# Two-layer relational graph network with a mixture-of-experts tail: the first node stage's side work moved to other steps

## The chip, the core and the metric

The kernel runs on one core of a Trainium2 chip. The core has five engines that run their own instruction streams and meet by semaphores: PE (TensorE, matrix products and transposes), DVE (VectorE), ACT (ScalarE), POOL (GpSimd) and SP (SyncE, which here only issues DMAs). SBUF is the on-chip memory of 128 partitions, PSUM the banks that PE writes. The metric is the device time of one execution in microseconds (us).

## The reference

Two relational graph convolutions over 10000 nodes of width 512 and 5000 edges, then an expert layer over each node. Cut to what matters:

```
def rgcn_gate_layer(x, row, col, edge_type, basis, att, gate_w, root, bias):
    w = jnp.einsum('rb,bio->rio', att, basis)          # 2 relations from 30 bases
    x_j = x[col]
    msgs = []
    for r in range(2):
        gate = jax.nn.sigmoid(x_j @ gate_w[r, :, 0])
        msgs.append(gate[:, None] * x_j @ w[r])
    msg = jnp.where((edge_type == 0)[:, None], msgs[0], msgs[1])
    agg = jax.ops.segment_sum(msg, row, num_segments=x.shape[0])
    return agg + x @ root + bias

n = layernorm(x)
h = relu(rgcn_gate_layer(n, src, dst, ..., layer 1)); x = x + rgcn_gate_layer(h, ..., layer 2)
x = x + experts(layernorm(x))                          # 2 shared, 8 routed (top 2)
```

## The kernel before

The kernel has five stages: node stage A, edge stage B (layer 1), node stage C, edge stage D (layer 2), and the expert stage in groups of 512 rows. Every product is made of three single-pass products of high and low parts, so each matrix operand is split: ACT writes the high part (`th`, `wrh`, `eh`), DVE the rest (`tl`, `wrl`, `el`).

**A node stage** has 79 steps, one for 128 rows (a tile). In step k of stage A, PE transposes tile k+1 (L1055), then multiplies tile k by `root` (twelve matmuls of 512 columns, L1035). ACT writes `th` of tile k+1 and the normalised `xn_a` of tile k+2. DVE writes `tl` of tile k+1 (L1309), adds the bias to the product of tile k-1 (`yout`, L1324) and takes the moments of tile k+4 (L1296); in odd steps it also aggregates the moments of a pair of tiles (L1300), from which POOL makes the scale and shift (`rstd`, `nmr`, function `pair_rstd`, L689 to L694) that ACT needs for `xn_a`. Stage C is the same without moments and scale. PE's product of tile k needs `tl` of tile k and the `yout` of tile k-2, whose PSUM bank it takes.

**Relation weights** are formed inside the node stages: in each odd step up to 63, PE combines the bases (`w_rows`, L1106), ACT copies the result out (`wevac`, L880), and SP loads the next 896 KB of bases and every fourth step stores the rows to DRAM. Behind the last store SP loads all of them as `wrl` (2048 KB, L517), and ACT and DVE split them, eight pieces, one each in steps 70 to 77 (`w_hi`, `w_lo`, L884 and L1375).

**An edge stage** has 21 pairs of 128 edge slots, sorted by relation. A pair runs through a pipeline: POOL gathers rows (`gx`, L738), DVE takes their moments (`edge_stats`, L1332), POOL makes the root (`edge_root`, L761), DVE the shift (`edge_shift`), ACT `xn_e`, DVE the gate's dot product (`edge_gate`, L1352), ACT the sigmoid and `eh`, DVE `el` (L1360), PE the turn (`edge_turn`, L1068: a product with the matrix `same` that adds edges with the same target and transposes at once) and the product with the relation's weights, ACT the message `msg`, POOL an adding scatter into DRAM (L753). Each scatter of a pair waits until those of the pair before have landed, because two pairs can hit the same row. The next node stage starts when all have landed.

The pipeline is filled inside the node stage: `lead_in` names node steps in which ACT and DVE also do a `pair_step(u)` with a negative u; -4 is the first with work (moments of pair 0), -3 adds the gate of pair 0 and moments of pair 1, -2 adds `same` and `el` of pair 0, -1 the turn of pair 0. Before they are at steps 72, 74, 76 and 78 (step 70 is in the list with u = -5, which has no work). A `pair_step` stands behind the node step's own work on each engine, so what waits in it holds the node step after it.

**Side work of stage A**: edge slots are sorted by records scattered to DRAM (POOL, 40 indirect DMAs). The slots' row numbers are then turned by PE (step 56), copied by DVE (57), stored and loaded again as one row in all partitions (`row_src`, POOL, 1344 KB, L732), and in steps 64 to 77 DVE compares three of 42 slots a step against those before (`find_repeats`, L1394), which `scatter_rows` (step 78) makes into the scatter's row numbers.

The order on each engine is the order of the code. `walk` writes steps 0 to 7 out, runs a loop of eight steps a round up to step 55, and writes the rest out; only written-out steps can carry side work. Buffers around the change: `yout` has two pairs of tiles, `xin` four, `basis_t` two.

Of the kernel before, what the change touches and what calls it, by code (L numbers as in the profile page):

```python
# [61 lines left out]
def gnn_moe_kernel(nc, x, src, dst, etype, basis, att, gate_w, root, bias,  # L62
# [21 lines left out]
    CS = P // 4  # L84
    TRASH = N
# [14 lines left out]
    with ctx:  # L100
# [356 lines left out]
        def _(sp):  # L457
# [26 lines left out]
            def step(st):  # L484
# [25 lines left out]
                if st.t.i is None and st.t.k == 2 * CS + 1:  # L510


                    for i in range(2):
                        sp.wait_ge(s_wst[i], 64 * (CS // 4) * (st.layer + 1))
                    if st.layer:
                        sp.wait_ge(s_mm, C0)
                    sp.dma_start(wrl[:, :, :].bitcast(F32), w_dram[st.layer].rearrange("m i o -> i m o")).then_inc(s_wl, 16)  # L517
# [117 lines left out]
        def _(pool):  # L635
# [88 lines left out]
            for g in range(pairs_done + 2, 31):  # L724
# [3 lines left out]
            pair_rstd(Pos(31))  # L728
# [48 lines left out]
            for g in range(32, NG - 1):  # L777
                pair_rstd(Pos(g))
            for u in range(3):
                gather(Pair(SB, u))  # L780
            for g in range(NG - 1, NG + 1):
                pair_rstd(Pos(g))
            for u in range(-4, 0):
# [38 lines left out]
        def _(act):  # L822
# [59 lines left out]
            def w_hi(layer, m):  # L882
                act.wait_ge(s_wl, 16 * (layer + 1))
# [29 lines left out]
            def step(st):  # L913
# [9 lines left out]
                if st.t.i is None:  # L923
# [3 lines left out]
                    if 70 <= st.t.k < 78:  # L927
                        w_hi(st.layer, st.t.k - 70)
# [98 lines left out]
        def _(pe):  # L1027
# [82 lines left out]
            def step(st):  # L1110
                a1 = later(st, 1)
                lead = lead_in(st)
                if st.phase == SA and st.t.i is None and st.t.k == 56:
# [129 lines left out]
        def _(dve):  # L1243
# [180 lines left out]
            def step(st):  # L1424
# [8 lines left out]
                if st.t.i is None:  # L1433
# [3 lines left out]
                    if st.phase == SA and st.t.k == 57:  # L1437
                        dve.wait_ge(s_turned, 1)
                        dve.tensor_copy(src_row16[:], bank[7][0:ET, 0:P]).then_inc(s_row16, 1)
                    if st.phase == SA and st.t.k == 64:  # L1440
# [3 lines left out]
                    if st.phase == SA and st.t.k == 78:  # L1444
                        scatter_rows()
                    if 70 <= st.t.k < 78:
                        w_lo(st.layer, st.t.k - 70)
# [196 lines left out]
```

## Time and profile before

| | us |
|---|---|
| median of 3 runs | 1728.37 |
| the runs | 1728.41, 1728.37, 1724.84 |
| the profiled execution | 1723.27 |
| its span in the trace | 1721.5 |
| PE busy | 1592.3 (92% of the span) |
| DVE busy | 914.5 (53%) |
| ACT busy | 724.4 (42%) |
| POOL busy | 504.7 (29%) |

The shares are means over all stages; a stage must be read from its own stretch of the trace. On the trace's clock stage A runs up to some 340 us, edge stage B to some 530, stage C to 828, stage D to some 1010 and the expert stage to the end. Releasers (what a wait ended with) are inferred from semaphore events, and "issue" is time in which an engine waited for nothing that the profile shows. On POOL, which issues the indirect DMAs, a wait for a landed DMA can appear so.

### The profile page before, as it was taken

To read this page: it belongs to the slowest core of one execution; us is meant where nothing else is said; L and a number is where in the kernel's file an instruction comes from. 1 tells how busy PE (TensorE), PEld (TensorE's weight loads), DVE (VectorE), ACT (ScalarE), POOL (GpSimd) and SP (SyncE) were. 2 spreads that over 40 slices of the span, in tenths; PEclk is the share of its full clock that TensorE was granted. 3 is DMA by queue.
4 is the path that set the end of the run, shared out by engine and by line. 5 is a ranking of instruction groups with operands and counts; after the bars stand their busy time and mean duration, and the time that the engine had idled before them with its cause. 6 is when DMAs were issued, how large, how long until landed. Compare 5 with 4: busy or idle time off the path is not lost. (4 is left out here: it accounts for less than half of the span.)

```text
span 1721.5 us, 24584 instructions
## 1 busy us (share of the span) xinstructions
PE 1592.3 (92%) x7903; PEld 1257.1 (73%) x7903; DVE 914.5 (53%) x2179; ACT 724.4 (42%) x1168; POOL 504.7 (29%) x559
## 2 busy tenths in 40 slices
PE   3998999798995999999999927999999999999998
PEld 2776777677783777777888715888888888888887
DVE  4554556877751333334755535556555654655543
ACT  2443444466651222222665515344444444444442
POOL 3682212457752000000467533112211311221100
PEclk9999999899997999999999958999999999999999
DMA  8998998367766999995777660132123112311201
GB/s 256 262 268 236 279 270 300 104 160 125 125 95 187 277 272 283 278 278 193 235 127 128 104 160 25 74 133 88 74 92 129 74 73 98 122 73 74 86 25 43
DMA packets 72234, 270.46 MB, mean 157 GB/s; under 512 B 12438, under 2 KB 12452, under 8 KB 57042
## 3 DMA queue, kind: packets, MB, share of 16 engines
q1 hardware_dynamic: 51714, 223.82, 40.5%
q0 software_dynamic: 20432, 45.57, 14.6%
q8 instruction: 42, 0.69, 0.2%
q14 instruction: 46, 0.38, 0.1%
HBM read 179.82 MB, written 89.48 MB: 156 GB/s over the span
## 5 line engine op out<-in xcount | busy, mean ns | idle before, releaser
L811 POOL TENSOR_TENSOR zr<-zr,xr 128x2048 f32<-128x2048 f32 (+1 forms) x19 | 89.2, 4695 | 395.4 <-DMA xr<-in_x 394.9
L839 ACT ACTIVATE th<-bank 128x512 fp32r<-128x512 f32 x158 | 94.4, 597 | 202.3 <-PE bank L1055 199.5
L1306 DVE SCALAR_TENSOR_TENSOR tl<-bank,th 128x512 fp32r<-128x512 f32 x79 | 54.6, 691 | 212.9 <-ACT th L839 212.9
L1035 PE MATMUL bank<-tth,w1h 128*128 128x512 f32 (+1 forms) x400 | 163.9, 410 | 0.1
L1035 PE MATMUL bank<-ttl,w1h 128*128 128x512 f32 (+1 forms) x400 | 156.4, 391 | 0.0
L1035 PE MATMUL bank<-w2h,gth 128*128 128x512 f32 x395 | 155.5, 394 | 0.5 <-DVE gtl L1520 0.3
L1035 PE MATMUL bank<-tth,w1l 128*128 128x512 f32 (+1 forms) x400 | 155.3, 388 | 0.0
L1035 PE MATMUL bank<-w2h,gtl 128*128 128x512 f32 x395 | 154.7, 392 | 0.0
L1035 PE MATMUL bank<-w2l,gth 128*128 128x512 f32 x395 | 154.3, 391 | 0.0
L1035 PE MATMUL bank<-root1h,th 128*128 128x512 f32 x316 | 134.8, 427 | 7.7 <-DVE yout L1324 7.1
L738 POOL DMA_INDIRECT gx<-y,dst_slot x42 | 46.2, 1100 | 301.9 <-ACT xn_e L857 286.6
L1035 PE MATMUL bank<-root2h,th 128*128 128x512 f32 x316 | 131.9, 418 | 0.6 <-issue 0.6
L1035 PE MATMUL bank<-root1l,th 128*128 128x512 f32 x316 | 127.2, 403 | 0.0
L1035 PE MATMUL bank<-root1h,tl 128*128 128x512 f32 x316 | 126.5, 400 | 0.0
L1035 PE MATMUL bank<-root2l,th 128*128 128x512 f32 x316 | 125.1, 396 | 0.0
L1035 PE MATMUL bank<-root2h,tl 128*128 128x512 f32 x316 | 123.9, 392 | 0.0
L1309 DVE TENSOR_TENSOR tl<-bank,th 128x512 fp32r<-128x512 f32 x79 | 54.5, 690 | 120.2 <-ACT th L839 120.2
L880 ACT ACTIVATE wevac<-bank 128x512 f32<-128x512 f32 x64 | 38.3, 598 | 186.8 <-PE bank L1106 184.2
L969 ACT ACTIVATE gel<-bank,b 128x512 f32<-128x512 f32 (+1 forms) x100 | 68.4, 684 | 106.9 <-PE bank L1035 106.8
L1324 DVE TENSOR_TENSOR yout<-bank,bias_b 128x512 f32<-128x512 f32 x158 | 107.4, 680 | 1.6 <-DMA y<-yout 1.6
L1068 PE MATMUL bank<-same,eh 128*128 128x256 f32 x336 | 85.1, 290 | 15.2 <-issue 10.3
L1520 DVE TENSOR_TENSOR gtl<-gsc,gth 128x512 fp32r<-128x512 f32 (+1 forms) x80 | 85.3, 1066 | 21.7 <-ACT gth L981 16.3
(201 smaller groups left out, 3790.6 us busy)
## 6 DMA issues: line engine op xcount, KB each, us to landing
basis_t<-in_gnn_basis SPq DMA_DIRECT2D x64, 896.0 KB
xin<-in_x SPq DMA_DIRECT2D x39, 512.0 KB
y<-yout SPq DMA_DIRECT2D x39, 512.0 KB
xin<-y SPq DMA_DIRECT2D x39, 512.0 KB
z<-yout SPq DMA_DIRECT2D x39, 512.0 KB
xr<-in_x SPq DMA_DIRECT2D x19, 1024.0 KB, 6.9
zr<-z SPq DMA_DIRECT2D x19, 1024.0 KB, 4.8
out<-zr SPq DMA_DIRECT2D x19, 1024.0 KB, 3.9
```

Source lines behind the costliest of these rows:

```text
L738: pool.indirect_dma_start(out=gx[:, e % 6, :], out_offset=None, in_=x if pr.phase == SB else y1, in_offset=bass.IndirectOffsetOnAxis(ap=ds ...
L811: pool.tensor_tensor(zq, zq, xr[:, q.mod(2), 0:n, :], ALU.add).then_inc(s_zx, 1)
L839: act.activation(th_a[:, s, :], tpb[s][:], f).then_inc(s_hi, 1)
L880: act.activation(wevac[:, u.mod(2), c.mod(2), :], wb[c.mod(2)][:], ACT.Copy).then_inc(s_wv, 1)
L969: act.activation(gel[:, u % 2, 0:n], outb[u % 2][:, 0:n], ACT.Gelu, bias=b1[:, c:c + 1]).then_inc(s_ge, 1)
L1035: ins = pe.matmul(out_ap, a(k), b(k), start=first, stop=last)
L1068: pe.matmul(o, eh[:, j, k * P:(k + 1) * P], m, start=j == 0, stop=False)
L1306: ins = dve.scalar_tensor_tensor(out=tl_a[:, s, :], in0=tpb[s][:], scalar=0.0, in1=th_a[:, s, :].bitcast(F32), op0=ALU.max, op1=ALU.subtract)
L1309: ins = dve.tensor_tensor(tl_a[:, s, :], tpb[s][:], th_a[:, s, :].bitcast(F32), ALU.subtract)
L1324: dve.tensor_tensor(yout[:, st.gg.mod(2), st.t.mod(2), :], outb[st.T.mod(2)][:], bias_b[st.layer][:], ALU.add).then_inc(s_y, 1)
L1520: dve.tensor_tensor(gtl[:, c, 0:n], source, gth[:, c, 0:n].bitcast(F32), ALU.subtract).then_inc(s_gl, 1)
```

## The change

All of it is in stage A and its like in stage C (same functions):

- row numbers are turned at step 34 and copied at 35; POOL's waits for them move with it, from pair 31's `pair_rstd` to pair 20's;
- repeats are compared in steps 42 to 55, `scatter_rows` is at 56;
- the leading steps of the edge pipeline are 59, 63, 67 and 78; POOL's first six gathers stand ahead of pair 31's `pair_rstd`;
- `wrl` is loaded in two parts, rows 0 to 111 at step 61 and the rest at 65, and split two pieces a step in steps 68 to 71;
- the loops end at step 31, so steps 32 to 55 are written out.

```
-            if st.t.i is None and st.t.k >= NT - 9 and (NT - 1 - st.t.k) % 2 == 0:
-                return (SB if st.phase == SA else SD), -1 - (NT - 1 - st.t.k) // 2
+            left = NT - 1 - st.t.k
+            if st.t.i is None and left in LEADS:      # {19: -4, 15: -3, 11: -2, 0: -1}
+                return (SB if st.phase == SA else SD), LEADS[left]
...
-            stop = 2 * CS - 8
+            stop = CS
...
-                if st.t.i is None and st.t.k == 2 * CS + 1:
+                if st.t.i is None and st.t.k in (2 * CS - 3, 2 * CS + 1):
+                    first, last = (0, EARLY) if st.t.k < 2 * CS else (EARLY, CS)
                     for i in range(2):
-                        sp.wait_ge(s_wst[i], 64 * (CS // 4) * (st.layer + 1))
+                        sp.wait_ge(s_wst[i], 64 * (CS // 4 * st.layer + last // 4))
...
-            for g in range(pairs_done + 2, 31):
+            turn_g = TURN_AT // 2 + 3
+            for g in range(pairs_done + 2, turn_g):
                 pair_rstd(Pos(g))
...
+            first_g = turn_g + 1
+            for left, u in LEADS.items():
+                last_g = min(NG, (NT - 1 - left + 3) // 2)
+                for g in range(first_g, last_g + 1):
+                    if u == -4 and g == last_g:
+                        for v in range(3):
+                            gather(Pair(SB, v))
+                    pair_rstd(Pos(g))
+                first_g = last_g + 1
                 ahead(SB, u)
...
-                    if 70 <= st.t.k < 78:
-                        w_hi(st.layer, st.t.k - 70)
+                    if W_SPLIT_AT <= st.t.k < W_SPLIT_AT + R * ISUB // 2:
+                        for m in range(2):
+                            w_hi(st.layer, 2 * (st.t.k - W_SPLIT_AT) + m)
...
-                    if st.phase == SA and 64 <= st.t.k < 78:
-                        find_repeats(3 * (st.t.k - 64), 3)
+                    if st.phase == SA and REPEATS_AT <= st.t.k < REPEATS_AT + ET // 3:
+                        find_repeats(3 * (st.t.k - REPEATS_AT), 3)
```

DVE at the leading step with u = -2, before (step 76, between the `yout` of its own step and the `tl` of the next). `same`, `el` and `scratch` are the pair's turn matrix, low part and gate product:

```order
L1324 TENSOR_TENSOR yout<-bank,bias_b_54 128x512
L1394 SCALAR_TENSOR_TENSOR msg,dups<-row_src,src_slot,ones_lower 128x128
L1394 SCALAR_TENSOR_TENSOR msg,dups<-row_src,src_slot,ones_lower 128x256
L1394 SCALAR_TENSOR_TENSOR msg,dups<-row_src,src_slot,ones_lower 128x128
L1375 TENSOR_TENSOR wrl<-wrl,wrh 128x512
L1370 TENSOR_SCALAR same<-row_src,src_slot 128x256 x2
L1343 SCALAR_TENSOR_TENSOR enmr<-emv,erstd 128x2
L1360 SCALAR_TENSOR_TENSOR el<-xn_e,gate,eh 128x512 x2
```

And the same place after the change (step 67), up to the step behind it:

```order
L1306 BN_STATS bn<-xin 128x6
L1310 BN_AGGR mv<-bn 128x2 x2
L1380 TENSOR_SCALAR same<-row_src,src_slot 128x256 x2
L1353 SCALAR_TENSOR_TENSOR enmr<-emv,erstd 128x2
L1370 SCALAR_TENSOR_TENSOR el<-xn_e,gate,eh 128x512 x2
L1357 TENSOR_LOAD rel
L1357 ISA x2
L1362 ISA
L1362 SCALAR_TENSOR_TENSOR scratch,logit<-xn_e,gatew_52 128x512 x2
L1342 BN_STATS ebn<-gx 128x6 x2
L1345 BN_AGGR emv<-ebn 128x2 x2
L1348 TENSOR_SCALAR erstd<-emv 128x2
```

The repeats and the `wrl` ahead of the pair's work are gone; a node tile's moments and aggregates stand there instead, since step 67 still has them.

ACT at the leading step with u = -3, before (step 74). `wrh` is a piece of the relation weights, `xn_e` the pair's normalised rows:

```order
L839 ACTIVATE th<-bank 128x512
L831 ACTIVATE xn_a<-xin,nmr,rstd 128x512
L884 ACTIVATE wrh<-wrl 128x512
L853 ACTIVATE xn_e<-gx,enmr,erstd 128x512 x2
L839 ACTIVATE th<-bank 128x512
```

After (step 63):

```order
L848 ACTIVATE th<-bank 128x512
L840 ACTIVATE xn_a<-xin,nmr,rstd 128x512
L889 ACTIVATE wevac<-bank 128x512
L862 ACTIVATE xn_e<-gx,enmr,erstd 128x512 x2
L848 ACTIVATE th<-bank 128x512
```

`xn_e` now stands behind `wevac`, which waits for PE's last matmuls of that step.

## Rows read from the trace of the kernel before

**Rows 1.** Windows: span, busy of PE, PEld, DVE, ACT, POOL, clock, DMA, GB/s

```profile
198.00:251.00 53.00, 53.00 (x288) 37.57 (x280) 28.17 (x56) 21.96 (x35) 10.08 (x29) 1.00 0.94 275
285.00:340.00 55.00, 47.45 (x214) 37.98 (x214) 49.38 (x155) 26.64 (x42) 20.15 (x33) 0.91 0.51 177
```

**Rows 2.** Timeline of PE, end of stage A: start, duration, instruction, [idle before, releaser]

```profile
277.37 0.60 PE L1055 MATMUL bank<-ident,xn_a 128*128 128x128 f32 x4
...
281.66 0.66 PE L1055 MATMUL bank<-ident,xn_a 128*128 128x128 f32 x4
285.23 0.63 PE L1055 MATMUL bank<-ident,xn_a 128*128 128x128 f32 x4
...
304.47 0.60 PE L1055 MATMUL bank<-ident,xn_a 128*128 128x128 f32 x4
304.82 0.47 PE L1035 MATMUL bank<-root1h,th 128*128 128x512 f32 x1
...
319.01 0.76 PE L1035 MATMUL bank<-root1h,th 128*128 128x512 f32 x1 [3.43 <-DVE yout L1324]
...
339.50 0.28 PE L1068 MATMUL bank<-same,eh 128*128 128x256 f32 x1
...
349.38 0.55 PE L1068 MATMUL bank<-same,eh 128*128 128x256 f32 x1 [3.13 <-DVE el L1360]
```

**Rows 3.** Timeline of DVE in the step that PE starts at 304.47

```profile
306.32 0.68 DVE L1309 TENSOR_TENSOR tl<-bank,th 128x512 fp32r<-128x512 f32 x1
...
308.40 0.45 DVE L1394 SCALAR_TENSOR_TENSOR msg<-row_src,src_slot,ones_lower 128x256 f32<-128x256 int16 x1
...
309.70 0.69 DVE L1375 TENSOR_TENSOR wrl<-wrl,wrh 128x512 fp32r<-128x512 f32 x1
310.30 0.68 DVE L1309 TENSOR_TENSOR tl<-bank,th 128x512 fp32r<-128x512 f32 x1
```

**Rows 4.** Timeline of DVE in the leading steps 72, 74 and 76

```profile
315.48 0.69 DVE L1332 BATCH_NORM_STATS2 ebn<-gx 128x6 f32<-128x512 f32 x1 [1.51 <-DMA gx<-in_x,dst_slot]
...
317.58 0.68 DVE L1309 TENSOR_TENSOR tl<-bank,th 128x512 fp32r<-128x512 f32 x1
...
327.44 0.69 DVE L1352 SCALAR_TENSOR_TENSOR scratch<-xn_e,gatew 128x512 f32<-128x512 f32 x1 [1.01 <-ACT xn_e L853]
...
330.47 0.68 DVE L1309 TENSOR_TENSOR tl<-bank,th 128x512 fp32r<-128x512 f32 x1
...
336.59 0.61 DVE L1370 TENSOR_SCALAR same<-row_src,src_slot 128x256 fp32r<-128x256 int16 x2
...
341.55 0.68 DVE L1309 TENSOR_TENSOR tl<-bank,th 128x512 fp32r<-128x512 f32 x1
```

**Rows 5.** Timeline of ACT, the weight rows of step 63

```profile
281.80 0.60 ACT L880 ACTIVATE wevac<-bank 128x512 f32<-128x512 f32 x1 [2.50 <-PE bank L1106]
```

**Rows 6.** Timeline of POOL: first and sixth gather, first and last pair's scatter

```profile
310.92 1.11 POOL L738 DMA_INDIRECT gx<-in_x,dst_slot  x1 [0.17 <-issue]
...
317.61 0.94 POOL L738 DMA_INDIRECT gx<-in_x,dst_slot  x1 [0.30 <-issue]
...
360.54 1.67 POOL L753 DMA_INDIRECT y<-msg,scat_slot  x1 [0.20 <-issue]
...
526.34 1.56 POOL L753 DMA_INDIRECT y<-msg,scat_slot  x1 [4.46 <-issue]
```

**Rows 7.** DMA issues (KB, us to landing); DVE's timeline beside the broadcast

```profile
row_src<-src_rows POOLq DMA_DIRECT2D x1, 1344.0 KB, 11.1
...
280.95 0.69 DVE L1324 TENSOR_TENSOR yout<-bank,bias_b 128x512 f32<-128x512 f32 x1 [1.63 <-DMA y<-yout]
```

**Rows 8.** Timeline of PE: start of stage C; first and second turn of stage D

```profile
536.82 1.94 PE L1055 MATMUL bank<-ident,xin 128*128 128x128 f32 x8 [20.49 <-DMA xin<-y]
...
827.68 0.28 PE L1068 MATMUL bank<-same,eh 128*128 128x256 f32 x1
...
833.25 0.36 PE L1068 MATMUL bank<-same,eh 128*128 128x256 f32 x1 [0.74 <-issue]
```

More of the change, by code:

```diff
@@ L84, in gnn_moe_kernel @@
     CS = P // 4
+    EARLY = 28
+    TURN_AT, REPEATS_AT, W_SPLIT_AT = 34, 42, 68
+    LEADS = {19: -4, 15: -3, 11: -2, 0: -1}
     TRASH = N
@@ L509, in step @@
                         store_w(st.layer, st.t.div(4))
-                if st.t.i is None and st.t.k == 2 * CS + 1:
+                if st.t.i is None and st.t.k in (2 * CS - 3, 2 * CS + 1):
+                    first, last = (0, EARLY) if st.t.k < 2 * CS else (EARLY, CS)
                     for i in range(2):
-                        sp.wait_ge(s_wst[i], 64 * (CS // 4) * (st.layer + 1))
+                        sp.wait_ge(s_wst[i], 64 * (CS // 4 * st.layer + last // 4))
                     if st.layer:
                         sp.wait_ge(s_mm, C0)
-                    sp.dma_start(wrl[:, :, :].bitcast(F32), w_dram[st.layer].rearrange("m i o -> i m o")).then_inc(s_wl, 16)
+                    rows = slice(4 * first, 4 * last)
+                    sp.dma_start(wrl[rows, :, :].bitcast(F32),
+                                 w_dram[st.layer].rearrange("m i o -> i m o")[rows]).then_inc(s_wl, 16)
             def store_pair(phase, g):
@@ L882, in w_hi @@
             def w_hi(layer, m):
-                act.wait_ge(s_wl, 16 * (layer + 1))
+                act.wait_ge(s_wl, 32 * (layer + 1))
                 act.activation(wrh[:, m, :], wrl[:, m, :].bitcast(F32), ACT.Copy).then_inc(s_wh, 1)
@@ L1112, in step @@
                 lead = lead_in(st)
-                if st.phase == SA and st.t.i is None and st.t.k == 56:
+                if st.phase == SA and st.t.i is None and st.t.k == TURN_AT:
                     pe.wait_ge(s_slots, 2)
@@ L1436, in step @@
                         dve.tensor_tensor(root2l[:], stage1[:], root2h[:].bitcast(F32), ALU.subtract).then_inc(s_rootl, 1)
-                    if st.phase == SA and st.t.k == 57:
+                    if st.phase == SA and st.t.k == TURN_AT + 1:
                         dve.wait_ge(s_turned, 1)
                         dve.tensor_copy(src_row16[:], bank[7][0:ET, 0:P]).then_inc(s_row16, 1)
-                    if st.phase == SA and st.t.k == 64:
+                    if st.phase == SA and st.t.k == REPEATS_AT:
                         dve.wait_ge(s_srcb, 16)
-                    if st.phase == SA and 64 <= st.t.k < 78:
-                        find_repeats(3 * (st.t.k - 64), 3)
-                    if st.phase == SA and st.t.k == 78:
+                    if st.phase == SA and REPEATS_AT <= st.t.k < REPEATS_AT + ET // 3:
+                        find_repeats(3 * (st.t.k - REPEATS_AT), 3)
+                    if st.phase == SA and st.t.k == REPEATS_AT + ET // 3:
                         scatter_rows()
-                    if 70 <= st.t.k < 78:
-                        w_lo(st.layer, st.t.k - 70)
+                    if W_SPLIT_AT <= st.t.k < W_SPLIT_AT + R * ISUB // 2:
+                        for m in range(2):
+                            w_lo(st.layer, 2 * (st.t.k - W_SPLIT_AT) + m)
                 if lead:
```

9 lines of the change are left out of this document (1 added, 8 removed).

## The prediction

> **What bounds the kernel now.** I read the windows first, then the timelines of PE, DVE, ACT and POOL around the one place where PE stops. PE is the bound through the first node stage: from 198 to 251 us it is busy 53.00 of 53.00 us, with the DMA engines at 0.94 [rows 1]. A step without weight rows takes 3.21 us (285.23 to 304.47 is six of them), one with them 4.29 (277.37 to 281.66) [rows 2]. There is nothing to win inside the stage, only at its end: from 285 to 340 us PE is busy 47.45 of 55 us and DVE 49.38 [rows 1]. Step 65 starts at 285.23. Thirteen steps of 3.20 would put the first edge turn (step 78) at 326.8; it stands at 339.50 [rows 2]. So 12.7 us are lost in steps 65 to 77. The second turn, at 349.38, is 9.9 behind the first [rows 2].
>
> Why: DVE's part of a plain step is 2.08 us with the aggregates, which only every second step has (306.32 to 308.40); three repeats take 1.30 and one wrl 0.60 [rows 3]. That is 3.8 to 4.0 in a step of 3.2, and the leading steps of the edge pipeline come on top: at 72 one that waits 1.51 for its gather, at 74 one of 3.03 behind a wait of 1.01, at 76 one of 4.96 [rows 4]. PE then waits for DVE, 3.43 us at the worst [rows 2]. Over these 55 us the granted clock is 0.91 [rows 1], that is 0.09 x 2 x 55 = 10 us at 1.2 instead of 2.4 GHz, which costs about 5 of the 12.7.
>
> Behind this stands a chain that the change doesn't touch. The first scatter is issued at 360.54, the first one of the last pair at 526.34: 20 pairs at 8.29 [rows 6], and each waits for the one before. The second node stage starts at 536.82, after 20.49 us of waiting for xin<-y, which is held for the last scatter [rows 8]. So what moves the first scatter moves all that follows, one for one.
>
> **The change part by part.** Times inside a step are counted from its start on PE.
>
> *Row numbers turned at 34, repeats at 42 to 55.* One PE transpose, one DVE copy and two POOL DMAs move by 22 steps and keep their distance from each other; POOL's wait for the copy now has pair 20's rstd behind it instead of pair 31's, at the same distance. In steps 42 to 55 DVE has 2.08 + 1.30 = 3.4 at most, in a mean step of 3.75 (half of 3.21 + 4.29): it fits, and since the aggregates stand ahead of the repeats, POOL and ACT are served as early as now. What is not free is the broadcast. It took 11.1 us to land, and a y store beside it held DVE for 1.63 us [rows 7], of which PE lost 0.36 (281.66 to 285.23 is 3.57 instead of 3.21) [rows 2]. It moves from where the basis loads end into the stretch at 0.94 DMA. Bounds: 0.4, as now, and 4.9 us, its 1344 KB at 275 GB/s [rows 1], if all of it were a delay. I take 0.9, near the lower end, because that row is the same DMA beside the same y store; so 0.5 more than now.
>
> The Trainium skill (DMA: Bandwidth & Descriptors, "Issuing engines are not separate DMA queues") says that transfers issued by any engine run on the same 16 DMA engines and interleave. It speaks against this part: that POOL issues the broadcast gives it no bandwidth of its own. By that rule, the trace agrees as far as the 1.63 us go; what it would make of the time is rival B.
>
> *Pipeline filled at 59, 63, 67 and 78.* Three leading steps leave the crowded end, and four steps lie between them, so DVE catches up. But each is a burst, and a burst beyond the slack stops PE. The slack: tl of the step that began at 304.47 starts at 306.32, one 0.60 operation late, so undisturbed 1.25 behind the start; yout ends 1.20 behind it; PE's product needs both 0.35 (304.82 less 304.47) behind the next start, 3.56 [rows 2, 3]. 3.56 - 1.25 - 1.20 = 1.1 us.
> - Step 59. The moments of pair 0 take DVE under 2.1 (315.48 to 317.58) and may wait: the gather was used 4.6 behind its issue at 310.92 [rows 4, 6], DVE asks for it some 5.6 behind, but with the DMA engines full it may take 8. The six gathers hold POOL for 7.7 us (310.92 to 317.61 and one more of 1) [rows 6]; pair 31's rstd behind them comes 2 late, and ACT's xn_a and PE's transpose take 0.5 of that. I put 1.0, between 0.5 and 4.
> - Step 63 still has weight rows, so ACT does wevac first, at 4.43 (281.80 less 277.37) [rows 2, 5], and xn_e only at 5.0. DVE's gate waits for xn_e, about 1.0 more, and the next tl comes 3.03 after the gate [rows 4]: at 9.0. Queued behind the waiting gate are tl and yout, and PE waits for both. Undisturbed, tl is at 4.29 + 1.25 = 5.5. Late by 3.5, less 1.1: PE stops 2.4, between 1.5 and 3.5.
> - Step 67. DVE is free at 1.25 + 2.08 = 3.33, the block from same to tl is 4.96 [rows 4]: tl comes at 8.3 instead of 3.21 + 1.25 = 4.46. ACT's table load lies beside it and may add 0.4. Less 1.1: PE stops 2.7 to 3.2; I take 3.0.
> - Clock. Now a stop of 3.43 us and its neighbours bring 10 us at the low level. The stop at 67 is nearly that, the one at 63 shorter. I take 3.4 us at the low level, a cost of 1.7; bounds 0 and 5, as now.
>
> What takes the place of the 12.7: 0.5 + 1.0 + 2.4 + 3.0 + 1.7 = 8.6. Gain up to the first turn: 4.1.
>
> *Step 78 on.* DVE comes there without backlog (now it carries three repeats, a wrl, four operations of scatter_rows and a late gate). The second layer has no repeats and shows the transition: its turns stand at 827.68 and 833.25, 5.6 apart with 0.74 idle [rows 8]. I take 5.3 here, against 9.9. Between second turn and first scatter DVE has gate, moments, same, tl, yout, el, gate and moments once more, and POOL an erstd. It took 11.2 (349.38 to 360.54) [rows 2, 6] with PE also late; I put 11.6, since now PE's turn is early and DVE's queue sets it. Together 16.9 instead of 21.0: gain 4.1.
>
> *Weights in two parts, used at 68 to 71.* Two wrl a step make DVE 2.08 + 1.20 = 3.3 at most in 3.2: level, so the backlog of step 67 is worked off from 72 on. The load of 2048 KB at 275 GB/s is 7.6 us or more; issued behind 285 as now it would land as step 68 begins at 295. The early part makes the wait 0. It puts 1.8 MB beside the y store of step 60; that is in the broadcast's range. The cost of both I take as 0.
>
> The Trainium skill (same page, "Rules for kernel authors") says "Don't bother" of two transfers to disjoint partition halves, since they share the same engines. By that the split is worth nothing in itself, and the sum has nothing for it; only the earlier start would count, and no row shows it alone.
>
> *Second layer.* The same steps without moments and rstd. At 63 two gates (3.03 less moments, about 1.5) behind the late xn_e bring tl to 7.2 instead of 5.5: 0.6 of stop. At 67 the block is about 3.4 from 2.45 on: tl at 5.8 instead of 4.46, 0.2. The transition can win up to the 0.74 [rows 8], I take 0.6. Net cost 0.2. *Shorter loops*: the same steps written out; no row shows a cost. 0.
>
> Sum: 4.1 + 4.1 - 0.2 = 8.0 us faster. The profiled execution took 1723.27 us (span 1721.5) and would take 1715.3. The median of three runs is 1728.37, and they lie 3.6 apart. From the median: 1720.4.
>
> **Rivals.**
> A. The stops at 60, 63 and 67 don't happen; they are sums of latencies over four engines, each of which I may have put too late. Then the 8.6 shrink to the broadcast's 0.5 and the second layer's 0.2 go: 16.3 faster, 1712.1. Against it stands a row for each term.
> B. The DMA engines become the bound from step 38 to 62. At 0.94 a pair of steps (7.5 us) leaves 0.45 us free; broadcast and six gathers are 2.9 MB, 10.5 us at 275 GB/s. Every pair whose y store lands late holds DVE as at 280.95 [rows 7]. If each of 11 pairs (steps 40 to 61) costs PE 1.2, that is 13 lost against 8 won: 1733, slower. It decides from 0.7 a pair. Against it: next to the broadcast PE lost only 0.36.
> C. Half of that, 4 to 7 lost: 1724 to 1728, no difference.
> D. The first scatter waits for something else, the last y store or a DMA behind the second layer's first basis loads; then only the first 4 us arrive: 1724.5.
>
> **How the numbers follow.** The forecast has 0.50, A 0.12, C and D together 0.24, B 0.14. A measurement of this kernel tells 0.2% (3.5 us) from no change. Faster by more: the forecast but for its lowest edge, and A, 0.60. Slower: B, 0.14. Within: 0.26. The range reaches to A and a little beyond, and over C to the near edge of B: 1710 to 1729.
>
> **What would show it.** Right: first turn near 335.4 on the trace's clock, second 5.3 behind, first scatter near 352.3, the second stage's start near 528.6; stops of PE of 2 to 3 us in the steps behind 63 and 67, ended by DVE yout or tl. Wrong: DVE yout waiting for y<-yout in several pairs between 180 and 280 us (B); no stops behind 63 and 67 (A); a first scatter that doesn't follow the second turn (D); PE waiting at step 34 for the slots, in which case the moved wait sets a new stop.

## The result, and the profile after

The changed kernel takes 1723.36 us (median of 20 runs) where the kernel before takes 1726.39 (median of 20): ratio 0.9979, 95% interval 0.9969 to 0.9989, so 3.6 us faster, between 1.9 and 5.4; the medians are 3.0 apart. A second set of 12 runs (a1 below) gave 0.9964 (0.9945 to 0.9983), or 6.2 us. Ratios leave out executions far off all others of their kernel, one of 3221 us in e1 (an experiment below) and one of 2026 us in before. The forecast was 8.0 us faster, 1720.4. The sign was right and the time lies in the range of 1710 to 1729; the size is 2.2 times too large by the first ratio and 1.3 times by the second, and the experiments show which terms of the sum were off.

The two windows of [rows 1], now of the changed kernel (columns: window, span, busy time and instructions of PE, PEld, DVE, ACT, POOL, granted clock, DMA share, GB/s):

```profile
198.00:251.00 53.00, 53.00 (x282) 37.62 (x281) 44.33 (x136) 22.67 (x35) 11.34 (x28) 1.00 1.00 290
285.00:340.00 55.00, 49.82 (x233) 39.76 (x230) 38.76 (x82) 27.91 (x44) 17.15 (x32) 0.94 0.50 161
```

DVE's repeats have moved: 28.17 to 44.33 us busy in the first window, 49.38 to 38.76 in the second. PE is still busy through all of the first, with the DMA share at 1.00 instead of 0.94. Yet in the second it has won only 2.4 us, 47.45 to 49.82. Where the rest stays shows in PE's timeline of the changed kernel (start, duration, instruction, and in brackets the idle time before it and what ended it): every stop between step 59 and step 69, the first two edge turns, and the step starts beside them.

```profile
169.65 0.60 PE L1065 MATMUL bank<-ident,xn_a 128*128 128x128 f32 x4
...
273.76 0.47 PE L1045 MATMUL bank<-root1h,th 128*128 128x512 f32 x1 [1.74 <-DVE yout L1334]
...
291.27 0.47 PE L1045 MATMUL bank<-root1h,th 128*128 128x512 f32 x1 [1.95 <-DVE yout L1334]
...
295.69 0.60 PE L1065 MATMUL bank<-ident,xn_a 128*128 128x128 f32 x4
...
306.47 0.63 PE L1065 MATMUL bank<-ident,xn_a 128*128 128x128 f32 x4 [1.00 <-ACT xn_a L840]
309.07 0.64 PE L1045 MATMUL bank<-root1h,th 128*128 128x512 f32 x1 [1.98 <-DVE yout L1334]
...
313.50 0.60 PE L1065 MATMUL bank<-ident,xn_a 128*128 128x128 f32 x4
...
339.47 0.28 PE L1078 MATMUL bank<-same,eh 128*128 128x256 f32 x1
...
344.58 0.36 PE L1078 MATMUL bank<-same,eh 128*128 128x256 f32 x1 [0.29 <-issue]
```

The three leading steps each stop PE behind them, ended by DVE's yout, as forecast; behind the third ACT's xn_a adds 1.00. The first turn is at 339.47; it was at 339.50 [rows 2]. But step 34 begins at 169.65 here and at 168.21 in before, 1.4 later, although up to there the kernels differ only in that steps 32 and 33 are written out; in the second trace of the changed kernel (a1) it begins at 168.40:

```profile
168.21 0.66 PE L1055 MATMUL bank<-ident,xn_a 128*128 128x128 f32 x4
```

So the traces are best compared from the start of step 34. Up to the first turn that is 171.3 us before and 169.8 after: 1.5 won, where the forecast had 4.1. From there the gain is 4.6, where the forecast had 4.1: the second turn is 5.1 behind the first instead of 9.9 (forecast 5.3), and the first scatter stands at 355.88 instead of 360.54 [rows 6], 16.4 behind the first turn instead of 21.0 (forecast 16.9). POOL's timeline of after, and two of its windows, around the clock's low stretches:

```profile
354.94 0.74 POOL L768 TENSOR_TENSOR erstd<-erstd,minus_half 128x2 f32<-128x2 f32 x1 [4.00 <-DVE erstd L1348]
355.88 1.67 POOL L760 DMA_INDIRECT y<-msg,scat_slot  x1 [0.20 <-issue]
```

```profile
290.70:298.90 8.20, 7.63 (x28) 6.09 (x29) 5.05 (x10) 1.30 (x2) 1.45 (x5) 0.79 0.88 282
308.40:313.60 5.20, 4.53 (x13) 3.56 (x14) 5.17 (x11) 1.19 (x3) 0.76 (x3) 0.67 0.63 205
```

The first scatter follows 0.20 us behind POOL's erstd, which had waited 4.00 us for DVE: DVE's queue sets it, not PE. In the second layer stage C is 1.2 us longer (from its first transpose to the first turn of stage D 292.1 instead of 290.9), with a stop of 0.39 behind its step 63 and one of 0.16 behind 67 that before has not, and the first turn of stage D to the first z scatter is 0.4 shorter:

```profile
784.71 0.47 PE L1045 MATMUL bank<-root2h,th 128*128 128x512 f32 x1 [0.39 <-DVE yout L1334]
```

### The profile page after: what moved, and what is told of

It reads as the page before. It is cut to its first block and busy times, and to the rows that moved or that the text cites. A ratio compares the mean times of both kernels' runs of the same rounds, so it can differ in the third digit from the quotient of the medians.

```text
span 1721.3 us, 23994 instructions
## 1 busy us (share of the span) xinstructions
PE 1591.4 (92%) x7903; PEld 1256.5 (73%) x7903; DVE 911.7 (53%) x2179; ACT 724.4 (42%) x1168; POOL 505.0 (29%) x559
## 5 line engine op out<-in xcount | busy, mean ns | idle before, releaser
L1078 PE MATMUL bank<-same,eh 128*128 128x256 f32 x336 | 83.8, 287 | 12.1 <-issue 10.1
L1531 DVE TENSOR_TENSOR gtl<-gsc,gth 128x512 fp32r<-128x512 f32 (+1 forms) x80 | 80.0, 1000 | 21.7 <-ACT gth L991 16.3
```

The lines of the kernel that those rows point to most:

```text
L1078: pe.matmul(o, eh[:, j, k * P:(k + 1) * P], m, start=j == 0, stop=False)
L1531: dve.tensor_tensor(gtl[:, c, 0:n], source, gth[:, c, 0:n].bitcast(F32), ALU.subtract).then_inc(s_gl, 1)
```

## How far one trace moves by itself

The profiled spans are 1721.5 before and 1721.3 after, nearly equal, although the stretch that was changed is 6.1 us shorter. Two runs of unchanged kernels say why: the changed kernel again (a1) and the kernel before again (b1, run last).

> The changed kernel once more, to see how far one profiled execution moves by itself. Theory: the gain sits between step 34 and the first scatter-add and repeats in every trace, 186.4 us from the turn of the row numbers to the first scatter-add (192.3 in before), with the two stretches of low granted clock in steps 64 to 70 again; the rest of the span (scatter chain 167.9 us in after against 165.8 in before) moves by a microsecond or two for no reason of the change. Ratio to before 0.998. Rival: the longer scatter chain is a cost of the change (167.9 again, to within 0.5 us, in every trace of the changed kernel).

> The kernel before once more, since all comparisons of stretches rest on one trace of it. Theory: stage A's loss and the transition belong to its order and repeat: step 56 to first turn 88.1 us and first turn to first scatter-add 21.0 us, each within 0.5 us (1.7 us where one more or one less stretch of low clock falls in), and the scatter chain lies anywhere between 164 and 169 us. Rival: the 21.0 us were one execution's bad luck, 17 to 19 here.

Measured, all in us from the timelines of PE (start of the transposes of step 34; first and second edge turn) and POOL (first scatter; first of the last pair). The table also holds the experiments that follow:

| kernel | step 34 to first turn | turn to turn | second turn to first scatter | step 34 to first scatter | first scatter to that of the last pair |
|---|---|---|---|---|---|
| before | 171.3 | 9.9 | 11.2 | 192.3 | 165.8 |
| b1, before again | 171.1 | 9.7 | 11.2 | 192.0 | 164.7 |
| after | 169.8 | 5.1 | 11.3 | 186.2 | 167.9 |
| a1, after again | 169.7 | 5.1 | 11.3 | 186.1 | 164.1 |
| e1, repeats only | 169.7 | 5.1 | 11.5 | 186.2 | 167.9 |
| e2, weights in one part | 168.5 | 5.1 | 11.3 | 184.9 | 164.7 |
| e3, repeats late | 174.9 | 5.3 | 11.2 | 191.4 | 165.3 |
| e4, even steps | 169.9 | 5.1 | 11.3 | 186.3 | 168.9 |
| e5, gathers early | 166.3 | 5.1 | 11.3 | 182.7 | 168.8 |
| e6, repeats 4 earlier | 170.4 | 5.9 | 11.2 | 187.4 | 166.5 |
| e7, spread | 162.5 | 5.1 | 11.3 | 178.9 | 166.0 |
| e8, spread, single gathers | 163.7 | 5.1 | 11.3 | 180.0 | 165.0 |
| e9, e1 with gathers early | 167.2 | 5.8 | 11.2 | 184.2 | 164.0 |
| e10, e4 with gathers early | 166.8 | 5.1 | 11.3 | 183.2 | 168.5 |

The stretch up to the first scatter repeats to 0.4 us in both kernels. Its parts move by more: steps 34 to 56 take 83.1 us in after and 83.8 in a1, where PE stops for 0.49 at 210.03, and the stop behind step 59 is 1.74 in after and 1.02 in a1. The chain of scatters behind it, which no edit touches, lies anywhere between 164.0 and 168.9 and was 167.9 and 164.1 in two traces of the same kernel. So an effect of a few microseconds can be read from one trace in the stretch where it arises, and not from the span. In before again the first turn to the first scatter is 20.8, so the 21.0 was no accident. The rivals of both runs fall. b1, e4, e5 and e6 were executed once each, so nothing is read from their times, only from their stretches.

## Experiments on the parts of the change

**e1: the repeats alone.** Before, with the turn at step 34 and the repeats at 42 to 55; leading pair steps and weights stay as they were.

```
     TURN_AT, REPEATS_AT, W_SPLIT_AT = 34, 42, 68
-    LEADS = {19: -4, 15: -3, 11: -2, 0: -1}
+    LEADS = {6: -4, 4: -3, 2: -2, 0: -1}
```

(against after; also w_hi and w_lo one a step at 70 to 77, one load of wrl, and the six gathers ahead of the rstd of pair 38)

> Before with the turn at step 34 and the repeats at steps 42 to 55; the leading pair steps and the weights stand as in before. Theory 1 (the repeats carried most of the 12.7 us that stage A lost in steps 65 to 77): stage A wins 7 to 9 us, the transition wins nothing (9.9 us between the first two turns), turn of the row numbers to first scatter-add about 184 us, time 7 to 9 us under before, ratio 0.9955, that is better than the whole change. Rival (the leading steps and the weight splits in steps 70 to 77 carried it, repeats only lay beside them): stage A wins at most 3 us, first scatter-add at 189 to 191 us after the turn, ratio 0.9985.

Ratio 0.9973 (0.9955 to 0.9990). Both were wrong. Stage A wins 1.6 us, less than the rival's limit of 3; the transition, of which both said that it would win nothing, wins 4.5. Up to the first scatter e1 is as long as the whole change, 186.2. Its PE timeline:

```profile
317.29 0.72 PE L1041 MATMUL bank<-root1h,th 128*128 128x512 f32 x1 [3.23 <-DVE yout L1330]
...
326.08 0.63 PE L1061 MATMUL bank<-ident,xn_a 128*128 128x128 f32 x4 [1.02 <-ACT xn_a L837]
328.66 0.77 PE L1041 MATMUL bank<-root1h,th 128*128 128x512 f32 x1 [1.95 <-DVE yout L1330]
```

The stops are those of before: 3.43 [rows 2] and 1.95 (at 331.90) in before, 3.23 and 1.95 here, with no repeat within 16 steps. So the leading steps stop PE also without the repeats beside them. What made the 3.23 stands in the timelines of e1, DVE's and ACT's first, then POOL's:

```profile
313.71 0.69 DVE L1338 BATCH_NORM_STATS2 ebn<-gx 128x6 f32<-128x512 f32 x1 [2.37 <-DMA gx<-in_x,dst_slot]
314.84 0.70 DVE L1338 BATCH_NORM_STATS2 ebn<-gx 128x6 f32<-128x512 f32 x1 [0.43 <-DMA gx<-in_x,dst_slot]
```

```profile
320.14 0.81 ACT L837 ACTIVATE xn_a<-xin,nmr,rstd 128x512 f32<-128x512 f32 x1 [5.44 <-POOL nmr L698]
```

```profile
309.42 1.11 POOL L743 DMA_INDIRECT gx<-in_x,dst_slot  x1 [0.17 <-issue]
...
316.26 0.95 POOL L743 DMA_INDIRECT gx<-in_x,dst_slot  x1 [0.30 <-issue]
318.13 0.57 POOL L693 TENSOR_SCALAR rstd<-mv 128x2 f32<-128x2 f32 x1 [0.92 <-DVE mv L1306]
```

DVE stands 2.8 us for gathered rows, with tl and yout queued behind it, and six gathers hold POOL from 309.42 to 317.2, ahead of an rstd that ACT's xn_a needs.

**e2: the weights in one part.** The changed kernel with one load of wrl at step 65 and one split a step at 70 to 77.

```
-                    if W_SPLIT_AT <= st.t.k < W_SPLIT_AT + R * ISUB // 2:
-                        for m in range(2):
-                            w_hi(st.layer, 2 * (st.t.k - W_SPLIT_AT) + m)
+                    if 70 <= st.t.k < 78:
+                        w_hi(st.layer, st.t.k - 70)
```

> The changed kernel with the relation weights loaded in one part and split one per step at steps 70 to 77 as before. Theory: the two-part load cost and gave nothing, so turn to first scatter-add is 186.4 us as in after, within 0.7 us, ratio to before 0.998. Rival 1: two splits a step at steps 68 to 71 stand behind the leading step 67 on ScalarE and VectorE and cost part of its 5.0 us stop: 2 us less, 184.4. Rival 2: one load late at step 65 runs into the last pairs' stores and loads and costs 1 to 2 us more.

Ratio 0.9969 (0.9954 to 0.9984), the same as the whole change; 184.9 us up to the first scatter, 1.3 under after. That is outside the 0.7 of the theory and near rival 1's 184.4, but not at rival 1's place. Against after, e2 spends 0.8 less behind step 59 (a stop of 0.92 instead of 1.74; a1 has 1.02), 1.6 less behind step 63, before any split, and 0.8 more behind 67. PE's timeline of e2, and then the windows of the stops behind 63 and 67:

```profile
289.09 0.47 PE L1042 MATMUL bank<-root1h,th 128*128 128x512 f32 x1 [1.95 <-DVE yout L1331]
291.92 0.60 PE L1062 MATMUL bank<-ident,xn_a 128*128 128x128 f32 x4
...
305.28 0.77 PE L1042 MATMUL bank<-root1h,th 128*128 128x512 f32 x1 [1.98 <-DVE yout L1331]
310.54 0.98 PE L1062 MATMUL bank<-ident,xn_a 128*128 128x128 f32 x4
```

```profile
288.50:295.20 6.70, 6.11 (x29) 5.05 (x30) 4.97 (x10) 1.42 (x2) 1.48 (x5) 1.00 0.77 234
305.00:310.60 5.60, 5.32 (x13) 4.13 (x14) 2.77 (x7) 0.00 (x0) 1.46 (x4) 0.50 0.49 172
```

The first of them is 1.95 us here and in after, in the same step. Here the clock stays at 1.00 and the next step's transposes come 2.83 us behind the product; in after the clock is 0.79 over the window, that is 3.4 us at 1.2 GHz, and they come 4.42 behind. That is 1.6 us for the same stop. The early part of the load, which stands ahead of this place, isn't what decides it: e5 below has it and keeps the full clock. The second stop, 1.98 in both, falls in a stretch at 1.2 GHz in both kernels, and costs 0.8 more here. So the two-part load neither cost nor gave anything that these runs can tell, as its term of 0 said.

**e3: the repeats back, the rest kept.** The changed kernel with the turn at 56 and the repeats at 64 to 77 (and the six gathers ahead of the store of the turned numbers).

```
-    TURN_AT, REPEATS_AT, W_SPLIT_AT = 34, 42, 68
+    TURN_AT, REPEATS_AT, W_SPLIT_AT = 56, 64, 68
```

> The changed kernel with the turn at step 56 and the repeats at steps 64 to 77 as before; the leading steps at 59, 63, 67 and the two-part weights stay. Theory 1: the 8 us of the repeats stay in stage A and about 9 us of the leading steps come on top of them, against a gain of 4.5 us in the transition: 3 to 5 us slower than before, ratio 1.002. Rival (what is lost in stage A is one amount for the leading steps and the repeats together, 12 us wherever they stand): 1 to 4 us faster than before, ratio 0.9985.

Ratio 1.0013 (0.9995 to 1.0032): no gain left. Theory 1's 1.002 lies in the interval, the rival's 0.9985 doesn't. Stage A loses 3.6 us against before (174.9 to 171.3), and the transition wins 4.6 all the same: turn to turn 5.3, with all repeats in their old place. PE stops nine times between step 59 and the first turn, in after five times; its timeline of e3, the longer ones:

```profile
281.22 0.63 PE L1064 MATMUL bank<-ident,xn_a 128*128 128x128 f32 x4 [2.40 <-ACT xn_a L839]
...
291.59 0.47 PE L1044 MATMUL bank<-root1h,th 128*128 128x512 f32 x1 [1.95 <-DVE yout L1333]
...
306.50 0.63 PE L1064 MATMUL bank<-ident,xn_a 128*128 128x128 f32 x4 [1.66 <-ACT xn_a L839]
309.32 0.76 PE L1044 MATMUL bank<-root1h,th 128*128 128x512 f32 x1 [2.19 <-DVE yout L1333]
...
326.81 0.63 PE L1064 MATMUL bank<-ident,xn_a 128*128 128x128 f32 x4 [1.55 <-ACT xn_a L839]
```

Of the transition e1 and e3 together say: it needs DVE to be without backlog at step 77. Taking the repeats out of the last steps (e1) is enough, and so is taking out the leading steps 72 to 76 (e3, where the weight splits leave steps 72 to 77 with them and the gathers stand earlier); doing both wins it only once.

**e6: how far the repeats must go.** e1 with `TURN_AT, REPEATS_AT, W_SPLIT_AT = 52, 60, 68`, so that they end at step 73, four steps earlier than in before.

> Before with the turn at step 52 and the repeats at steps 60 to 73 (scatter rows at 74), that is only four steps earlier; leads and weights as in before. From the first run: the transition's 4.5 us come from taking the repeats out of steps 77 and 78, not from the leading steps. Theory: first turn to first scatter-add 16.5 us (21.0 in before), stage A keeps its loss (turn of the row numbers at step 52 to first turn 102 to 104 us; before would be 103.2 from step 52). Rival: the whole removal of the repeats from the leading steps is needed: 19 to 21 us from first turn to first scatter-add.

Close to the theory: 17.0 us from first turn to first scatter, 102.4 from the turn of the row numbers to the first turn. Four steps bring 4.0 of the 4.6 us of the transition. DVE's timeline of e6 from step 77 on shows what is no longer in the way:

```profile
340.60 0.68 DVE L1381 TENSOR_TENSOR wrl<-wrl,wrh 128x512 fp32r<-128x512 f32 x1
...
341.80 0.61 DVE L1376 TENSOR_SCALAR same<-row_src,src_slot 128x256 fp32r<-128x256 int16 x2
...
342.39 1.29 DVE L1321 TENSOR_TENSOR tl_b<-bank,th_b 128x512 fp32r<-128x512 f32 x2
343.59 1.41 DVE L1366 SCALAR_TENSOR_TENSOR el<-xn_e,gate,eh 128x512 fp32r<-128x512 f32 x2
```

In before three repeats stood ahead of that wrl and the four operations of scatter_rows ahead of that same, and PE's second turn waited 3.13 us for the el [rows 2]; here el begins 4.4 us behind the first turn.

## Experiments on what stops PE

**e4: leading steps on even steps.** The changed kernel with them at 58, 62, 66, where no wevac stands ahead of ACT's xn_e.

```
-    LEADS = {19: -4, 15: -3, 11: -2, 0: -1}
+    LEADS = {20: -4, 16: -3, 12: -2, 0: -1}
```

> The changed kernel with the leading pair steps at 58, 62, 66 in place of 59, 63, 67 (even steps have no copy of basis weights on ScalarE); the rest of the change stays. Theory: behind step 63 xn_e waited for that copy (VectorE idle 2.15 us), so the second stop falls from 1.95 to about 1 us, its stretch of low clock goes too and 2.5 to 3 us are won: turn of the row numbers to first scatter-add 183.5 us (186.3 and 186.2 in the two traces of after). Rival: VectorE's own 5.3 us of leading work behind lo, y_out and the statistics sets the stop, 186.

186.3, the rival's number, but behind the second leading step the theory was right: its stop fell from 1.95 to 0.52 (and 0.44 for xn_a), the granted clock is 1.00 there, and the steps behind it are 1.3 us longer than undisturbed ones instead of 4.0. What this gave was lost elsewhere. The stop of 1.41 in step 66 stands behind a yout that waited 2.39 us for a y store, as DVE's line below shows, and made that step 2.2 us longer. The third leading step costs 6.5 us, with waits of 2.09 for xn_a and 1.55 for yout, instead of 5.0. Stage C, where DVE has no moments to do, took 290.8 us here and 292.1 and 292.0 in after; that fits a gain, but e8, spread too, has 292.8, so C varies by as much.

```profile
283.78 0.47 PE L1045 MATMUL bank<-root1h,th 128*128 128x512 f32 x1 [0.52 <-DVE yout L1334]
...
292.43 0.47 PE L1045 MATMUL bank<-root1h,th 128*128 128x512 f32 x1 [1.41 <-DVE yout L1334]
...
301.34 1.05 PE L1065 MATMUL bank<-ident,xn_a 128*128 128x128 f32 x4 [2.09 <-ACT xn_a L840]
303.95 0.77 PE L1045 MATMUL bank<-root1h,th 128*128 128x512 f32 x1 [1.55 <-DVE yout L1334]
```

```profile
291.59 0.69 DVE L1334 TENSOR_TENSOR yout<-bank,bias_b 128x512 f32<-128x512 f32 x1 [2.39 <-DMA y<-yout]
```

**e5: gathers early.** The changed kernel with the first six gathers in twos ahead of the rstd of pairs 26, 27 and 28.

```
-                    if u == -4 and g == last_g:
-                        for v in range(3):
-                            gather(Pair(SB, v))
+                    if g in GATHER_AT:
+                        gather(Pair(SB, GATHER_AT.index(g)))
```

> The changed kernel with the first six gathers issued in pairs ahead of the rstd of tile pairs 26, 27 and 28 (steps 50 to 54) in place of six in a row ahead of that of pair 31. Theory: the loss behind step 59 (2.28 us: VectorE waits 3.6 us for gathered rows, POOL's rstd of pair 31 stands behind six gathers) goes to 0.3 or less, the stops behind 63 and 67 stay: turn to first scatter-add 184.2 us. Rival: six gathers among the basis loads delay loads or stores by themselves, the 2 us come back as waits in steps 50 to 56: 186.

182.7, 3.5 us under after (forecast 2.0 to 2.1). PE no longer stops behind step 59; its waits between step 34 and the first turn (in all, times, longest) are nearly all behind 63 and 67:

```profile
PE bank L1045 <- DVE yout L1334: 3.9, 2, 2.0
PE bank L1065 <- ACT xn_a L840: 1.4, 3, 1.0
```

The stop behind 59 was worth 2.3 us. The 1.95 stop behind 63 stays and here too is followed by full clock (the next transposes 2.83 us behind the product), which is another 1.6 us; whether the edit brings it isn't shown, since e2 has it without the edit. Between steps 34 and 56 this kernel takes 83.6 us, 0.5 more than after.

**e9 and e10: the same two edits in other company.** e9 is e1 with the gathers early (behind the rstd of pairs 26, 27, 28); e10 is e4 with them early.

> Before with the repeats at steps 42 to 55 (first run of this study, 169.8 us from the turn of the row numbers to the first turn) and the first six gathers issued in twos ahead of nothing, behind the rstd of pairs 26, 27 and 28; the leading pair steps stand at 72, 74, 76, 78 as in before, the weights too. Theory: there the stop of 3.23 us is VectorE's wait for gathered rows (2.37 and 0.43 us) and rstd behind six gathers; with these gone 3 to 5 us are won with their stretch of low clock, 165 to 167, transition 16.6, time 3 to 4 us under after although no step leads early. Rival: at two steps' distance the leading steps press on each other, 169 or more.

> The changed kernel with leading steps at 58, 62, 66 and the first six gathers in twos ahead of the rstd of pairs 26, 27 and 28 (each alone: 170.1 and 166.4 us from the turn of the row numbers to the first turn, 169.9 and 169.8 in after). Theory: a whole leading step of 5.3 us on VectorE costs a stop of 1.4 to 2 us wherever it stands, so 165.5 to 167.5, 3 to 5 us above the spread kernel. Rival: the even steps' run was only disturbed by its y stores (10.4 us of VectorE's waits), without them the step-63 stop goes too: 163.

e9 took 0.9955 (0.9937 to 0.9973) of before's time, e10 0.9966 (0.9947 to 0.9985). To the first turn e9 needs 167.2, just above the theory's 167, and e10 166.8, inside its theory. PE's timeline of e9: the 3.23 stop has gone to 0.23, the second one is as it was.

```profile
318.96 0.47 PE L1040 MATMUL bank<-root1h,th 128*128 128x512 f32 x1 [0.23 <-DVE yout L1329]
...
327.72 0.63 PE L1060 MATMUL bank<-ident,xn_a 128*128 128x128 f32 x4 [1.59 <-ACT xn_a L836]
330.30 0.77 PE L1040 MATMUL bank<-root1h,th 128*128 128x512 f32 x1 [1.95 <-DVE yout L1329]
```

So e9, which fills the pipeline at steps 72 to 78 as before, is as fast as the change or faster. The two stops belong to the leading steps 72 and 74. The third leading step, the largest, stands at step 76 and costs nothing ahead of the first turn: step 77 takes its 3.2 us, and PE has the turn to do before it needs that DVE work (in e1 it is the same, 0.3 us). In after the same work at step 67 costs 5.0. PE's timeline of e10, behind its second and third leading steps:

```profile
282.44 0.47 PE L1045 MATMUL bank<-root1h,th 128*128 128x512 f32 x1 [0.52 <-DVE yout L1334]
...
297.55 0.63 PE L1065 MATMUL bank<-ident,xn_a 128*128 128x128 f32 x4 [1.86 <-ACT xn_a L840]
300.16 0.60 PE L1045 MATMUL bank<-root1h,th 128*128 128x512 f32 x1 [1.98 <-DVE yout L1334]
```

e10's time lies in its theory, but the theory's reason, a stop of 1.4 to 2 us wherever a leading step stands, doesn't hold. The second stops PE for 0.52 us again, now without a late y store beside it: on an even step, where xn_e doesn't stand behind wevac, it costs 1.4 us, against 2.4 in e5, which has the same clock there. The third costs 5.8, against 4.8 in e5, and the steps up to the turn lose another 0.7. Why the third is dearer on an even step is open.

**e7: every leading step but the last taken apart.** One or two pieces a step between 57 and 72, half a pair each; gathers early; weights split at 70 to 77.

```
+    LEADS = {0: -1}
+    PARTS = [(57, "stat", 0, 0), (58, "stat", 0, 1), (60, "shift", 0, 0), (60, "xn", 0, 0), (61, "gate", 0, 0),
+             (59, "stat", 1, 0), (62, "stat", 1, 1), (62, "xn", 0, 1), (63, "gate", 0, 1), (64, "shift", 1, 0),
+             (64, "xn", 1, 0), (65, "stat", 2, 0), (65, "xn", 1, 1), (66, "gate", 1, 0), (66, "gated", 0, 0),
+             (67, "stat", 2, 1), (67, "gated", 0, 1), (68, "gate", 1, 1), (69, "lo", 0, 0), (70, "lo", 0, 1),
+             (71, "same", 0, 0), (72, "same", 0, 1)]
...
+        def parts(st, do):
+
+            if st.t.i is None:
+                for k, kind, u, j in PARTS:
+                    if k == st.t.k and kind in do:
+                        do[kind](Pair(SB if st.phase == SA else SD, u), (j,))
```

(columns: step, piece, pair, half; each helper of the pair step takes the halves that it is to do)

> The changed kernel with every leading pair step but the last taken apart: one or two pieces of a pair a step between 57 and 72 (statistics, shift, normalised rows, gate, gated rows, lower parts, equality, each half a pair), gathers early (two each ahead of the rstd of pairs 25, 26, 27), weights split one a step at 70 to 77. Theory: what stage A lost (11.7 us) was the length of a leading step on VectorE in one PE step; taken apart it fits, so turn of the row numbers to first turn is 158 to 160 us (169.8), to first scatter-add 175; in the second layer stage C is 1 us shorter, time 10 to 13 us under after, ratio to before 0.991. Rival: VectorE has no room in steps 64 to 77 (3.2 us each) and loses 0.3 to 0.5 us a step: first turn 165, ratio 0.994.

1711.93 us, ratio 0.9908 (0.9876 to 0.9940), the forecast 0.991; it beats both kernels. No run compares it with after directly; by the ratios to before it takes 0.993 to 0.994 of after's time. The windows, and PE's waits between step 34 and the first turn (329.92), all that are left:

```profile
198.00:251.00 53.00, 51.58 (x269) 36.68 (x268) 42.71 (x131) 22.57 (x35) 16.96 (x33) 1.00 1.01 313
285.00:329.00 44.00, 42.92 (x210) 34.00 (x209) 33.63 (x70) 25.05 (x39) 14.93 (x28) 1.00 0.53 172
```

```profile
PE bank L1078 <- ACT xn_a L852: 2.3, 5, 0.7
```

There is no stop ended by yout, and the granted clock is 1.00 to the turn. But the first turn comes 162.5 behind step 34, above the 158 to 160 of the theory and under the rival's 165. Of that 1.8 us lie before step 56 (85.1 us from 34 to 56, 83.3 in before), where DVE waits 2.0 and 2.2 us for y stores and the early gathers run at a DMA share of 1.01. Behind step 56 PE waits 1.0 us, and the steps there are 2.2 us longer in all than undisturbed ones. Taking the steps apart isn't the whole of e7's gain: to the first turn it is 7.3 us ahead of after, and e5, with early gathers and whole leading steps, is already 3.5 ahead. The other 3.8 are the pieces and the clock that stays up; the weights, one split a step again, were worth nothing in e2.

**e8: e7 with single gathers,** each behind another rstd (pairs 23 to 28 and 34 to 37).

> The spread kernel of the run before (162.7 us from the turn of the row numbers to the first turn), with its first ten gathers issued one at a time, each behind the rstd of one tile pair (pairs 23 to 28, 34 to 37). Theory: its remaining 2.3 us of TensorE waits in steps 51 to 72 come from gathers in twos that hold up y stores (VectorE waited 2.0 and 2.2 us for y<-yout) and rstd; one at a time they cost under 1 us: 160.5 to 161.5, ratio to before 0.990. Rival: y stores are late by themselves, as in the run with even steps (10.4 us of waits for them in all with gathers in a row), whatever the gathers do: 162 to 163.5.

Ratio 0.9938 (0.9916 to 0.9960), 163.7 us: the rival's reason, and its 163.5 just passed. The gathers' grouping is not what holds the stores: DVE's waits for them grew, and the first stands at 198.53, ahead of the first gather at 210.15. DVE's waits of e8 between step 34 and the first turn, and the one stop of PE that a late store made (DVE's yout ahead of it had waited 2.35 for it):

```profile
DVE yout L1348 <- DMA y<-yout: 13.3, 11, 2.4
```

```profile
292.38 0.46 PE L1059 MATMUL bank<-root1h,th 128*128 128x512 f32 x1 [1.45 <-DVE yout L1348]
```

The same line has 7.5 us in e7, 3.9 in after, 10.4 in e4 and 0.8 in e5. These waits come and go between kernels with the same stores, and what decides them stays open. Short ones DVE's slack takes; long ones reach PE: 1.63 us made a step of before 0.36 longer [rows 2, 7], 2.35 and 2.39 stop PE for 1.4 here and in e4. e7 and e8 can't be told apart by their intervals.

## Why the prediction was half right

- *Broadcast, +0.5: measured 0 to 0.5.* Steps 34 to 56 take 83.1 us in after and 83.8 in a1, 83.3 in before, and the 0.36 us that it cost beside step 64 is gone. Of rival B its sign is seen and not its price: DVE waits for a y store in four pairs between 198 and 221 us, which the text had named as the sign of B, but PE doesn't stop once between step 34 and step 59 of after, and only for the 0.49 us in a1 (DVE's waits of after between step 34 and the first turn: total, times, longest):

```profile
DVE yout L1334 <- DMA y<-yout: 3.9, 6, 0.9
```

  That the DMA share was 0.94 already was little reason for a loss; DVE's slack took nearly all of the late stores. With early gathers in the same stretch steps 34 to 56 take 83.3 (e10), 83.6 (e5), 84.3 (e8), 84.6 (e9) and 85.1 us (e7). The rule of the Trainium skill (DMA: Bandwidth & Descriptors, "Issuing engines are not separate DMA queues"), that the transfers of all issuing engines share the same 16 DMA engines, isn't contradicted: the share rose from 0.94 to 1.00, but nobody on the path waited in after.
- *Step 59, 1.0: measured 2.3.* The mechanism was right, the gather's landing too short: DVE waited 2.92 and 0.72 us for rows whose gathers were issued at 261.29 and 262.71, a landing of over 8 us. The bound of 8 was in the text, with no row behind it, and I took the value nearest to the row of a lightly loaded stretch. In a1 the stop is 1.02 and the cost 1.5.
- *Steps 63 and 67, 2.4 and 3.0: measured 2.4 and 3.3 without the clock, and 0.35 more at step 73.* tl begins 8.9 and 8.8 us behind its step's start (289.85 and 307.65); the text had 9.0 and 8.3 to 8.7. Adding up DVE's queue by rows of before worked to 0.3 us.
- *Clock, 1.7: measured 3.4.* Two stretches of 3.4 us at 1.2 GHz (0.21 x 2 x 8.2 and 0.33 x 2 x 5.2 by the windows above) instead of one, in after and in a1. No row stood behind the 3.4; that it fits each stretch is luck as far as the text goes. e2 and e5 have the same 1.95 us stop with full clock behind it, so this term can't be forecast from the stop's length.
- *The sum of stage A, 8.6 in place of 12.7: measured 11.7 (2.3 + 4.0 + 5.0 + 0.35; the two middle ones with their clock).* Gain 1.5 instead of 4.1: 1.0 from these, and 0.5 from step 64 and steps 34 to 56. So the steps that failed are the clock, 1.7 too small, and the gather's landing at step 59, 1.3 too small. Behind the sizes stands a reason that was wrong too: that the crowding of repeats and leading steps made the 12.7. e1 shows the same stops without a repeat near them, and e9 equals the change with the bursts close together. What a burst costs depends on its place: the first one's stop was mostly the gathers' (3.23 in e1, 0.23 in e9); the second costs 2.4 us at full clock behind wevac and 1.4 on an even step (e5, e10); the third, 5 us of work against 1.1 of slack, costs 4.8 to 6.5 at steps 66 and 67, where the change puts it, and 0.3 or nothing at 76 (e1, e9), where it stood before. e7, which keeps each piece under the slack, has steps 2.2 us longer in all behind step 56.
- *Transition, 4.1: measured 4.6, and the reason holds.* DVE comes to step 78 without backlog. The text gave this to the leading steps and the repeats as one; e1 and e3 show that moving either is enough, e6 that moving the repeats four steps nearly is. That DVE's queue sets the first scatter was right: POOL's erstd ends 0.20 us ahead of it in after, e1, e6 and e7 alike.
- *Weights, 0: right.*
- *Second layer, 0.2 cost: 0 to 0.8.* Stage C took 292.1 and 292.0 us in the traces of after, 290.9 and 291.6 in those of before; the transition won 0.4.
- *Sum, 8.0.* In the traces 6.1 up to the first scatter, less up to 0.8 in the second layer; by the two ratios 3.6 and 6.2. The second stage, forecast to start near 528.6, starts at 534.42 in after and at 529.20 in a1. The chain from the first scatter on passed no gain or loss of its own that stands out of its spread of some 4 us.

One point is open and wasn't tried: since POOL's erstd of pair 4 stands ahead of the first scatter and waits some 4 us for DVE, the scatter could perhaps go first.

## What to carry to other kernels

Work that is squeezed into the slack of a busy engine's partner must be measured per step against that slack. Here moving bursts that exceed it gave and took: a place where the burst waits for less made its stop shorter, and the place behind which PE has other work cost nothing, until the change gave it up. Taking them apart removed the stops ended by yout. Before moving several things at once, try them singly: moving the repeats alone (e1) gave all of the 6.1 us up to the first scatter, and moving them four steps 4.9 of them. And issue gathers by the landing time under the load that they will meet, from a queue on which nothing urgent stands behind them.

## What was not expected of the hardware

- The same stop of TensorE, 1.95 us in the same step, was followed by full clock in e2 and e5 and by 3.4 us at 1.2 GHz in after and a1; the cost differs by 1.6 us.
- 1344 KB of broadcast in a stretch where the DMA engines were at 0.94 cost TensorE nothing in after and 0.5 us in a1. Late stores did stop it where DVE waited 2.39 and 2.35 us for one: by 1.41 in e4 and 1.45 in e8.
- A gather that was used 4.6 us behind its issue under half load took over 8 us to land beside the loads of stage A.
- A chain of 20 dependent scatter pairs took between 164.0 and 168.9 us in 14 traces without any edit to it.
